# Spreading the combination of routed rows over the last three dense groups, and moving six casts from ScalarE to VectorE

## What is computed

```python
x = x + attention(layernorm(x))           # pooled query, pooled key, Wt
h = rmsnorm(layernorm(x)) * norm_weight
shared = relu(h @ sw1 + sb1) @ sw2 + sb2  # 256 -> 1024 -> 256, all tokens
probs = sigmoid(h @ router_w.T)           # 8 experts, the best 2 of each token
routed = sum over the two of weight * (relu(h @ ew1[e] + eb1[e]) @ ew2[e] + eb2[e])
x = x + shared + routed
```

## Time and profile before

| | us |
|---|---|
| median of 3 runs | 732.78 (730.52 to 733.04) |
| the profiled execution | 730.89 |
| its span, first to last instruction | 729.1 |
| PE busy | 710.0 (97%) |
| DVE busy | 565.2 (78%) |
| ACT busy | 433.7 (59%) |
| granted TensorE clock | 1.00 in all 40 slices |

### The profile page before, as it was taken

How to read it: one execution, slowest core, us unless ns; L and a number is a source line. 1 busy time by engine, 2 the same in 40 slices (tenths; PEclk the granted TensorE clock), 3 DMA queues, 4 the chain that set the end, 5 groups by cost and what they waited for, 6 DMA issues and landing times. The chain is left out here.

```text
span 729.1 us, 11314 instructions
## 1 busy us (share of the span) xinstructions
PE 710.0 (97%) x4084; PEld 586.5 (80%) x4084; DVE 565.2 (78%) x1124; ACT 433.7 (59%) x731; POOL 182.5 (25%) x155
## 2 busy tenths in 40 slices
PE   8899899999999999999999999999999999999997
PEld 6446575877888988898888889988988889888786
DVE  6626686998966868896788598968877888767994
ACT  3631445355448677578657685668585775866522
POOL 1100101000004333434345334533342643121000
PEclk9999999999999999999999999999999999999999
DMA  8500122030002646655566455745654766424960
GB/s 287 218 2 1 58 95 79 1 120 4 2 1 67 204 152 218 219 187 170 175 216 227 142 174 195 242 148 176 218 159 143 196 225 208 142 81 140 341 204 29
DMA packets 46184, 106.92 MB, mean 147 GB/s; under 512 B 9421, under 2 KB 34000, under 8 KB 38576
## 3 DMA queue, kind: packets, MB, share of 16 engines
q1 hardware_dynamic: 39312, 88.49, 37.3%
q0 software_dynamic: 6816, 17.71, 7.4%
HBM read 89.39 MB, written 17.69 MB: 147 GB/s over the span
## 5 line engine op out<-in xcount | busy, mean ns | idle before, releaser
L986 ACT ACTIVATE hid<-psU,b 128x512 f32<-128x512 f32 (+2 forms) x280 | 152.5, 579 | 128.7 <-issue 76.2
L708 PE MATMUL psD<-w,hhi 128*128 128x512 f32 x824 | 214.9, 400 | 2.4 <-DVE x_sb L1378 1.1
L708 PEld LDWEIGHTS psD<-w,hhi 128*128 128x128 f32 x824 | 147.5, 188 | 33.4 <-ACT hhi L989 2.6
L1334 DVE TENSOR_TENSOR hlo<-hid,hhi 128x512 fp32r<-128x512 f32 x206 | 138.2, 691 | 44.9 <-ACT hhi L989 42.8
L1384 DVE TENSOR_TENSOR w<-raw,w 128x1024 fp32r<-128x1024 f32 x112 | 133.3, 1218 | 2.6 <-ACT w L878 2.1
L430 POOL DMA_INDIRECT token_out<-fold,dst x71 | 89.5, 1260 | 168.2 <-DVE fold L1378 162.4
L422 POOL DMA_INDIRECT xin<-token_in,src x71 | 79.3, 1116 | 208.9 <-DVE src L1579 105.3
L684 PE MATMUL psU<-xhl,w 128*128 128x512 f32 (+1 forms) x448 | 124.8, 360 | 0.3 <-DVE xhl L1241 0.3
L678 PE MATMUL psU<-xhl,w 128*128 128x512 f32 (+1 forms) x448 | 124.5, 359 | 0.0
L680 PE MATMUL psU<-xhl,w 128*128 128x512 f32 (+1 forms) x448 | 124.1, 358 | 0.0
L714 PEld LDWEIGHTS psD<-w,hlo 128*128 128x128 f32 x824 | 111.3, 188 | 11.0 <-DVE hlo L1334 1.7
(11 more groups left out here) (213 smaller groups left out, 591.0 us busy)
## 6 DMA issues: line engine op xcount, KB each, us to landing
raw<-in_wpack SPq DMA_DIRECT2D x58, 1024.0 KB, 5.6
xT<-token_out SPq DMA_DIRECT2D x32, 256.0 KB, 4.6
token_in<-z_sb SPq DMA_DIRECT2D x8, 512.0 KB, 3.5
out<-x_sb SPq DMA_DIRECT2D x16, 256.0 KB, 4.9
b<-in_b2pack SPq DMA_DIRECT2D x29, 128.0 KB, 5.0
x_sb<-in_x SPq DMA_DIRECT2D x6, 512.0 KB, 7.8
xin<-token_in,src POOLq DMA_INDIRECT x71, 3.7
token_out<-fold,dst POOLq DMA_INDIRECT x71, 4.5
```

The lines of the kernel that those rows point to most:

```text
L708: mm(acc, hhi[:, part], wpair[slot][:, :, c * D:(c + 1) * D], start=(c == 0), stop=False)
L986: last = nc.scalar.activation(hid[:, n % 4, i * rows:(i + 1) * rows], acc, ACT.Relu, bias=b1[:, u % 2, m:m + 1])
L1334: V.tensor_tensor(hlo[:, part], hid[:, n % 4, :], hhi[:, part].bitcast(F32), ALU.subtract).then_inc(hlo_ready, 1)
```

## The change

DVE's order and its share of the casts change in D1, D2 and D3; nothing before them does. The new list `high_by_dve` says for every step of every group whether DVE casts hhi. For the groups before D1 it says what the conditions before it said; in D1, D2 and D3 it is true for steps 3 and 7. There ACT leaves L989 out, DVE does the cast of L1330, and PE waits for `hhi_ready` instead of `hid_ready` for that step.

The combinations are called at other places. Behind each quarter stands one pair. In the up stages of D2 and D3 one more stands behind each two steps, for the first three pairs of steps, as long as fewer than 13 are done. So pairs 0 to 3 stand behind the quarters of D1, 4 to 6 in the up stage of D2, 7 to 10 behind its quarters, 11 and 12 in the up stage of D3, and 13, 14 and 15 behind its first three quarters. The wait of `combine` on `out_done` is now for the tiles of this pair that are already summed.

```diff
--- before.py
+++ after.py
@@ -302,7 +302,8 @@
         slot_of = [nth[g] + {"A": 0, "B": NA, "C": NA + NBT}[kinds[g]] for g in range(SA, SA + SLOTS)]
         unit_of = [{"A": 4 * nth[g], "B": 4 * NA + 2 * nth[g], "C": 4 * NA + 2 * NBT + nth[g]}[kinds[g]]
                    for g in range(SA, SA + SLOTS)]
-        casts = [4 + sum(2 * nrow[f] for f in range(g) if kinds[f] in "BC") for g in range(NG)]
+        high_by_dve = [j < 4 if g == 0 else kinds[g] in "BC" or (g >= SA + SLOTS and j % 4 == 3) for g in range(NG) for j in range(2 * nrow[g])]
+        casts = [sum(high_by_dve[:i + 1]) for i in range(L0[NG - 1] + 2 * nrow[-1])]
         QX = Q0[SA + SLOTS] - Q0[SA]
         rows_of_side = [sum(nrow[SA + i] for i in range(j + 1) if i % 2 == j % 2) for j in range(SLOTS)]
 
@@ -698,12 +699,11 @@
 
                     def high(c):
                         if q == 0 and c * rows % 512 == 0:
-                            if g == 0 and c < 4:
-                                pe.wait_ge(hhi_ready, c + 1)
-                            elif nrow[g] == 4:
-                                pe.wait_ge(hid_ready, G0[g] + c + 1)
+                            j = c * rows // 512
+                            if high_by_dve[L0[g] + j]:
+                                pe.wait_ge(hhi_ready, casts[L0[g] + j])
                             else:
-                                pe.wait_ge(hhi_ready, casts[g] + c * rows // 512 + 1)
+                                pe.wait_ge(hid_ready, G0[g] + j + 1)
                         part = slice(c * rows + q * P, c * rows + (q + 1) * P)
                         mm(acc, hhi[:, part], wpair[slot][:, :, c * D:(c + 1) * D], start=(c == 0), stop=False)
 
@@ -985,7 +985,7 @@
                     acc = psU[:, n % 4, i * rows:(i + 1) * rows]
                     last = nc.scalar.activation(hid[:, n % 4, i * rows:(i + 1) * rows], acc, ACT.Relu,
                                                 bias=b1[:, u % 2, m:m + 1])
-                    if rows == 512 and (g or j >= 4):
+                    if rows == 512 and not high_by_dve[L0[g] + j]:
                         last = nc.scalar.activation(hhi[:, j * 512:(j + 1) * 512], acc, ACT.Relu,
                                                     bias=b1[:, u % 2, m:m + 1])
                 last.then_inc(hid_ready, 1)
@@ -1326,9 +1326,9 @@
                 n = G0[g] + (j + 2 if kinds[g] == "C" else j)
                 part = slice(j * 512, (j + 1) * 512)
                 dve.wait_ge(hid_ready, n + 1)
-                if nrow[g] < 4 or (g == 0 and j < 4):
+                if high_by_dve[L0[g] + j]:
                     V.tensor_copy(hhi[:, part], hid[:, n % 4, :]).then_inc(hhi_ready, 1)
-                    dve.wait_ge(hhi_ready, (casts[g] if g else 0) + j + 1)
+                    dve.wait_ge(hhi_ready, casts[L0[g] + j])
                     if kinds[g] == "C":
                         dve.wait_ge(down_done, Q0[g])
                 V.tensor_tensor(hlo[:, part], hid[:, n % 4, :], hhi[:, part].bitcast(F32),
@@ -1617,10 +1617,11 @@
                 finish(g)
 
             def combine(n, summed):
+                t = min(2 * n + 2, summed)
 
                 r = n % RING
                 dve.wait_ge(token_rows[r], 32 * (n // RING + 1))
-                dve.wait_ge(out_done, Q0[SA + SLOTS] + max(0, 2 * n + 2 - 4 * SA) if summed else 4 * SA)
+                dve.wait_ge(out_done, Q0[SA + SLOTS] + t - 4 * SA if t > max(2 * n, 4 * SA) else 4 * SA)
                 for k in range(2):
                     for i in range(2):
                         t = 2 * n + i
@@ -1631,15 +1632,19 @@
 
             done = 0
             for g in range(SA + SLOTS, NG):
-                hidden(g)
+                for first, last in ((0, 2), (2, 4), (4, 6), (6, 8)):
+                    lows(g, first, last)
+                    if first < 2 * min(3, g - SA - SLOTS + 1 + (g == SA + SLOTS + 1)) and g > SA + SLOTS and done < 13:
+                        combine(done, 4 * nth[g])
+                        done += 1
                 if g + 1 < NG:
                     turned_lo(g + 1)
                 for q in range(4):
                     if 2 * done > 4 * nth[g] + q:
                         dve.wait_ge(combined, 4 * nth[g] + q + 1)
                     out_rows_of(g, q)
-                    while done < NT // 2 and done < 2 * (4 * (g - SA - SLOTS) + q + 1):
-                        combine(done, 2 * done + 2 <= 4 * nth[g] + q + 1)
+                    if done < NT // 2:
+                        combine(done, 4 * nth[g] + q + 1)
                         done += 1
```

## The result

| | before | changed |
|---|---|---|
| median of 10 runs, us | 731.48 (730.52 to 735.72) | 728.28 (727.58 to 731.14) |
| profiled execution, span, us | 729.1 | 726.1 |
| D1's up stage to D3's last quarter, us | 66.94 | 64.28 |

The ratio is 0.996, 95% interval 0.9947 to 0.9973: 0.4% faster, within 0.5%. Forecast were 729.4 us and 2.4 us of gain. The third line is the stretch by which the experiments are compared: from the first matmul of D1's up stage to the start of D3's quarter 3. Everything behind its end took 6.5 to 6.6 us in all twelve profiles of this case, and nothing before its start was changed. Profiled twice, the changed kernel gave 64.28 and 64.27 us; the kernel before was profiled once.

A forecast was written before the change was run, and what follows sets the result against it. PE, busy 97% of the span, was taken as the bound, with 3.37 us of stalls to win from D1 on. Terms 0.40 + 0.2 + 0.71 + 1.13 = 2.4 us, from 731.8, gave 729.4 us, range 727.3 to 732.3.

The forecast's parts named there:

- The four places: PE stalls from D1 on: D1's last two quarters 0.40, D2's quarter 0 1.13, D2's last two 0.71, D3's quarter 0 1.13 us.
- D1's quarters: With one pair per quarter DVE takes 2.37 us against PE's 2.78, so the 0.40 us stall goes.
- D2's quarter 0: After D2's up stage: 3.91 us becomes 3.7, only 0.2 of 1.13 won, as pair 6 stands where the last subtractions are due.
- my sequence: Step-by-step DVE schedule for D2's up stage: first subtraction 680.65, pairs 4 to 6 between, last subtraction 691.45 to 692.15.
- D2's quarters: DVE catches up by D2's quarter 2, so the 0.71 us stall goes and D3 starts at 700.8 instead of 702.06.
- D3's quarter 0: With two pairs in D3's up stage quarter 0 takes 2.8 us, the 1.13 goes, some 0.3 us in hand.
- The sum: Gains from D1 on: 0.40 + 0.2 + 0.71 + 1.13 = 2.4 us.
- Operations that overlap: DVE combinations start 0.396 us apart with a length of 0.479, so a pair was priced at 1.585 us.
- rival 3: DVE operations don't overlap in the mixed order: a pair costs 1.92 us, only 0.5 us won, 731.3 us; chance 0.04.
- The slower rival: Rival 4: DVE bounds the up stages, hid's four buffers fill; 1 us more per pair gives 734.1 us; chance 0.05.
- The absolute time: Mean 731.8 us of the four shown runs less 2.4 us gives 729.4 us.
- rival 1: More is won: D2's quarter 0 comes out without a stall, all 3.37 us goes, 728.4 us; chance 0.08.

The follow-up runs named there:

- the kernel with narrow combinations: Kernel before with each combination operation cut from 256 columns to 8, waits, loads and stores kept; stretch 63.55 us, median 728.58 us, ratio 0.9959.
- the third pair in D3: Changed kernel with `done < 14` instead of `done < 13`, so pair 13 stands in D3's up stage; stretch 65.00 us, ratio 0.997.
- the kernel with three more operations: Changed kernel with three extra DVE operations into an idle buffer behind each of the five up-stage pairs; stretch 71.71 us, ratio 1.0054.
- the kernel without casts: Changed kernel with the combinations in the new order but ACT writing hhi as before; stretch 63.55 us, median 727.88 us, ratio 0.9952.

## Why the prediction was right

- *The four places.* All four measured as listed: the kernel with narrow combinations took 3.39 us away, 3.37 was the sum of the list. DVE's time for the combinations, by which it fell behind 1.18 us a quarter, was the cause.
- *D1's quarters*, 0.40 forecast: D2 starts 22.11 us behind D1 instead of 22.52, 0.41.
- *D2's quarter 0*, 0.2 forecast: 0.39 measured. This term was mis-sized. I took 0.65 us for a subtraction from a row of six, but that row hides a wait. In narrower windows of the same trace its first five subtractions start 0.60 us apart, the fifth at 688.89, and the sixth only at 689.73:

```profile
686.49 1.89 DVE L1334 TENSOR_TENSOR hlo<-hid,hhi 128x512 fp32r<-128x512 f32 x3
...
689.73 0.69 DVE L1334 TENSOR_TENSOR hlo<-hid,hhi 128x512 fp32r<-128x512 f32 x1
```

In the mixed order each costs 0.60 to 0.61 as well. So the last subtraction of D2 starts 13.54 us behind the start of the up stage (690.87 - 677.33), where my sequence has 13.74 (691.45 - 677.71). That sequence was itself rounded low: its terms add up to 691.57, and by them only 0.1 us would have been won. That pair 6 stands where the last subtractions are due was right, as the third pair in D3 showed. Unseen was how cheap the remedy is: I had costed the casts between +0.9 and -0.2 us and not asked what the change would be without them.

- *D2's quarters*, 0.71 forecast: 8.33 instead of 9.05, 0.72.
- *D3's quarter 0*, 1.13 forecast: 2.80 instead of 3.91, 1.11. DVE had 0.3 us in hand by my sum; it had 0.86, since the third pair in D3 took 1.58 us and cost 0.72.
- *The sum*, 2.4 forecast: 2.66 in the stretch. The span fell by 3.0; the other 0.37 lies ahead of D1 (655.22 against 655.59), where nothing was changed: scatter, not gain.
- *Operations that overlap.* A pair took 1.58 us in the mixed order too (682.19 to 683.77), and rival 3 fell. Against the strict reading of "The DRAIN you can't avoid" in the Trainium skill's "VectorE: DVE Perf Modes" the trace decides: the next operation starts before the one before it has ended.
- *The slower rival.* Its mechanism, full hid buffers, did not appear even with 2.77 us a pair. Dearer pairs do make the kernel slower, but by the last subtraction and, beyond the sum, by PE's clock. The price was too low: by its sum, 0.79 and 1.19 us more a pair would make the stretch 1.3 and 3.2 us longer than before. Measured were 3.0 and 4.8, but 2.5 and 2.3 of that belong to the half clock; without it the price would have been too high.
- *The absolute time*, 729.4 forecast, 728.28 measured: half of the difference is the mean of the four runs of before (731.8 where ten runs gave a median of 731.48) and the term above. The other half is luck: the medians differ by 3.20 us, the stretch by 2.66, and the rest lies where nothing was changed. For the same reason it says nothing that the median lies at the 728.4 of rival 1: the stall in D2's quarter 0 that would be gone by that rival is still there, 0.72 us of it.

## What to carry to other kernels

When a second engine serves PE and has side work, put the side work where its wait is longest and count its time per stage of PE: here some 10.5 us (680.26 to 691.48, less 0.71 of waiting) in a stage of 10.99 still cost 0.73, because the first piece of its main work comes late and the last is due at the end. Work moved to an engine for balance must be priced again whenever that engine's order changes: the casts gained 1.20 us with the old order and lost 0.73 with the new one. A merged row of a timeline can hide a short wait, so the cost of one operation is better taken from a shorter row: 0.65 us here was 0.60 and one wait. Where the effect is smaller than the scatter of whole runs, compare the length of an affected stretch in the trace, which repeated within 0.01 us.

## What the runs showed of the hardware

A stall of PE can cost more than its length. Waits of 2.44 and 3.33 us in a dense stretch were followed by a granted clock of 0.50 and 2.2 to 2.3 us of extra matmul time. The clock was already down when the matmuls began again (in the kernel with three more operations it was 1.00 up to 693.0 and 0.50 from 693.5 on, and PE's wait ended at 694.23). The losses of 1.13 us in the kernel before consist of short waits, the longest listed 0.24 us, and the clock stayed at 1.00. It also stayed there behind a wait of 0.56 us in D3 of the kernel with three more.

The clock also has a part in the scatter between executions. Early in the kernel, among the first scores of the attention, it was at 1.00 in some executions and half of that in others: from 20 to 27 us the mean was 0.54 to 0.59 in four of the twelve profiled executions, 0.95 in one and 1.00 in seven. The first row is of the changed kernel, the second of the kernel without casts, the third of the changed kernel again (columns as above):

```profile
20.00:27.00 7.00, 5.32 (x42) 2.64 (x43) 5.48 (x25) 4.07 (x9) 1.64 (x1) 1.00 1.01 408
```

```profile
20.00:27.00 7.00, 5.96 (x26) 1.91 (x25) 3.57 (x19) 2.10 (x5) 1.64 (x1) 0.55 1.02 410
```

```profile
20.00:27.00 7.00, 5.30 (x43) 2.70 (x43) 5.47 (x25) 3.75 (x9) 1.64 (x1) 1.00 1.02 414
```

The second reached D1 at 657.80 instead of 655.22, 2.6 us later; 0.4 of it stood before the clock fell (the same matmuls start at 17.57 instead of 17.20), and 2.2 came while it was down. Ahead of this PE waits for DVE and ACT between short bursts: the longest wait was 1.14 us in the first and 1.67 in the second. But that difference by itself is not what tips the clock. The third had the wait of 1.67 us too, and one of 1.45 before it, and its clock stayed at 1.00; it reached D1 at 656.79, 1.6 us later than the first, and all of this stood by the end of these waits (18.75 instead of 17.20). What tips the clock here stays open.

A wait on the operation issued just before is not free on DVE: in D3, pair 14 waits for the sum ahead of it and starts 0.53 us behind its start, where 0.35 is the rule (pair 13 waits for older sums). Pair 15 waits like pair 14 and is as late, 720.23 to 720.76. The rows of pairs 13 and 14:

```profile
714.68 0.42 DVE L1378 TENSOR_TENSOR x_sb<-psD,x_sb 128x256 f32<-128x256 f32 x1
715.03 1.66 DVE L1630 SCALAR_TENSOR_TENSOR x_sb<-xT,top,x_sb 128x256 f32<-128x256 f32 x4
...
717.46 0.42 DVE L1378 TENSOR_TENSOR x_sb<-psD,x_sb 128x256 f32<-128x256 f32 x1
717.99 1.67 DVE L1630 SCALAR_TENSOR_TENSOR x_sb<-xT,top,x_sb 128x256 f32<-128x256 f32 x4
```
